# A four-layer Perceiver on one core: where the turned maxima sit in PSUM, and how the queries for the maxima are laid out

## The reference, cut to what matters

```
q = norm(x) @ Wq + bq;  k = ctx @ Wk + bk;  v = ctx @ Wv + bv        (16 heads of 16)
x = x + softmax(q k^T / 4 over 12544 keys) v @ Wo + bo
```

## Time and profile before

| | us |
|---|---|
| median of 3 runs | 1688.18 (1687.93 to 1692.31) |
| profiled execution, its own time | 1688.73 |
| its span, first to last instruction | 1686.9 |
| TensorE matmul busy | 1578.0 (94%) |
| TensorE weight loads busy | 1362.0 (81%) |
| VectorE busy | 1045.9 (62%) |
| ScalarE busy | 964.8 (57%) |
| GpSimd busy | 697.7 (41%) |

### The profile page before, as it was taken

The page is one execution under the profiler, slowest core; times in us unless marked ns, Lnnn a source line. Parts: engine busy times, 40 slices in busy tenths (PEclk is TensorE's granted clock), DMA queues, the critical chain, the costliest instruction groups (busy, mean ns, idle before and its releaser), DMA issues. The chain is left out here.

```text
span 1686.9 us, 48994 instructions
## 1 busy us (share of the span) xinstructions
PE 1578.0 (94%) x20162; PEld 1362.0 (81%) x20179; DVE 1045.9 (62%) x1445; ACT 964.8 (57%) x1848; POOL 697.7 (41%) x627
## 2 busy tenths in 40 slices
PE   6999999999887999999999987998799999999988
PEld 5888888888666889888898765986588898898863
DVE  7667777786346877777777343045676666666622
ACT  4677777777413466656656712352367777777742
POOL 5655555551004655554554000000375555555202
PEclk9999999999977999999999999999999999999998
DMA  7665555554234766555555352971475555555430
GB/s 180 166 198 131 120 140 131 132 123 106 65 116 116 183 182 170 143 145 138 137 147 126 88 207 85 362 256 51 127 175 140 138 128 120 140 133 132 100 108 4
DMA packets 149248, 235.65 MB, mean 140 GB/s; under 512 B 24200, under 2 KB 64516, under 8 KB 148100
## 3 DMA queue, kind: packets, MB, share of 16 engines
q1 hardware_dynamic: 141090, 225.29, 50.6%
q10 hardware_dynamic: 7938, 7.23, 1.7%
HBM read 107.26 MB, written 0.23 MB: 64 GB/s over the span
## 5 line engine op out<-in xcount | busy, mean ns | idle before, releaser
L1305 DVE TENSOR_REDUCE L_xattn_maxima<-L_xattn_ps 128x4 f32<-128x1024 f32 x588 | 691.6, 1219 | 327.3 <-PE L_xattn_ps L877 323.2
L1067 ACT ACTIVATE L_xattn_p_ring<-L_xattn_ps 128x512 f32<-128x512 f32 x1176 | 674.9, 599 | 340.8 <-PE L_xattn_ps L926 325.7
L926 PE MATMUL L_xattn_ps<-L_xattn_q_packed,L_xattn_k_packed 128*128 128x256 f32 x2352 | 452.1, 298 | 10.0 <-ACT L_xattn_p_ring L1067 5.0
L926 PEld LDWEIGHTS L_xattn_ps<-L_xattn_q_packed,L_xattn_k_packed 128*128 128x128 f32 x2352 | 335.3, 190 | 71.6 <-issue 35.9
L962 PE MATMUL L_xattn_ps<-L_xattn_p_ring,L_xattn_v_ring 128*17 128x128 f32 x9408 | 289.3, 273 | 1.0 <-ACT L_xattn_p_ring L1067 1.0
L962 PEld LDWEIGHTS L_xattn_ps<-L_xattn_p_ring,L_xattn_v_ring 128*17 128x17 f32 x9408 | 242.4, 97 | 23.6 <-ACT L_xattn_p_ring L1067 1.6
L845 PE MATMUL L_xattn_ps<-L_xattn_ctx_halves,L_xattn_w_halves 128*128 128x256 f32 x1764 | 260.9, 286 | 0.5 <-POOL L_xattn_ctx_halves L1224 0.4
L849 PE MATMUL L_xattn_ps<-L_xattn_w_halves,L_xattn_ctx_halves 128*128 128x256 f32 x1764 | 260.4, 286 | 0.0
L1239 POOL TENSOR_TENSOR L_xattn_k_ring<-L_xattn_k_full,consts 128x512 fp32r<-128x512 f32 x147 | 155.5, 1058 | 223.0 <-ACT L_xattn_k_full L1080 111.6
L1221 POOL TENSOR_TENSOR L_xattn_ctx_halves<-L_xattn_ctx_chunk,consts 128x512 fp32r<-128x512 f32 x129 | 134.4, 1042 | 263.1 <-DMA L_xattn_ctx_chunk<-in_ctx_chunks 178.9
L845 PEld LDWEIGHTS L_xattn_ps<-L_xattn_ctx_halves,L_xattn_w_halves 128*128 128x128 f32 x1764 | 233.3, 193 | 3.7 <-issue 1.8
(11 more groups left out here) (385 smaller groups left out, 1173.2 us busy)
## 6 DMA issues: line engine op xcount, KB each, us to landing
L_xattn_k_packed<-L_xattn_k_ring SPq DMA_DIRECT2D x588, 128.0 KB, 2.4
L_xattn_ctx_chunk<-in_ctx_chunks SPq DMA_DIRECT2D x147, 256.0 KB, 3.2
L_xattn_k_packed<-L_xattn_k_ring SPq DMA_DIRECT2D x588, 64.0 KB, 2.2
L_ffn_W<-in_experts_W SPq DMA_DIRECT2D x16, 1024.0 KB, 13.7
L_xattn_mask_chunk<-L_xattn_mask ACTq DMA_DIRECT2D x49, 128.0 KB, 3.0
weights<-in_pack_L_attn SPq DMA_DIRECT2D x10, 512.0 KB, 4.3
L_xattn_ctxT<-in_ctxT SPq DMA_DIRECT2D x5, 896.0 KB, 12.9
L_xattn_ctx<-in_ctx SPq DMA_DIRECT2D x5, 896.0 KB, 11.8
```

What stands on the lines that cost most here:

```text
L926: last = pe.matmul(L.ps[:, bank, d * 2 * S:(d + 1) * 2 * S], self.k_packed[s][:, quarter, d, half * P:(half + 1) * P], q[:, 2 * pair:2 * p ...
L1067: act.activation(self.p[t % P_RING][:, 4 * quarter:4 * quarter + 4, :], L.ps[:, E_BANK[unit], :].rearrange("p (h n) -> p h n", n=S), ACT.Exp)\
L1305: dve.tensor_reduce(out[:, 4 * v:4 * v + 4], L.ps[:, M_BANK + 2 * v:M_BANK + 2 * v + 2, :] .rearrange("p b (k n) -> p (b k) n", k=2), AX_X ...
```

## The change

1. `q_hi` and the packed source `q_pairs` hold four heads' worth (two for each block of eight) in place of 16. Within a strip's 32 rows only two heads lie, so a 0/1 column that keeps every even (or every odd) head, `pair16`, serves all four strips at once. VectorE's two products shrink from 128 x 1024 to 128 x 256, ScalarE's sixteen copies to four, its copy of 128 x 2048 to 128 x 512. The matmuls read the same numbers. The DMAs that pack the queries keep number and bytes.
2. In the turn steps from 9 to 45 of each layer (ten, `borrows(step)`) turned maxima and factor leave banks 0 and 1 and go to banks 2 and 3, where the first half of a maxima batch lies. They wait until VectorE has reduced the first half of that step's batch 0; batch 1 of the step waits until ScalarE has read the factor.
3. In those steps `pe_factor` moves from behind all six matmuls of `pe_project` part 3 to behind the first three; in all steps from 6 to 48 part 3 is issued in two calls of three. ScalarE takes the factor's exp right after unit 5 and before `act_drain_v`, not after it.

```diff
-          ("head16", 8), ("head32", 4), ("neg_half", 1), ("fill", P), ("turned", 1), ("turn_sign", 1)]
+          ("head16", 8), ("head32", 4), ("pair16", 2), ("neg_half", 1), ("fill", P), ("turned", 1), ("turn_sign", 1)]
...
+        "pair16": p[:, None] // 16 % 2 == np.arange(2)[None, :]
...
+def borrows(step):
+    return LAG <= step < NCHUNK
...
     def unit(key, step):
+        if key[0] != "scores" and borrows(step):
+            before.append(-1)
+            at[key] = len(at)
+            bank.append(M_BANK if key[0] == "turned" else M_BANK + 1)
+            return
...
-        self.q_hi = sb("q_hi", [P, H, S], F32R)
+        self.q_hi = sb("q_hi", [P, 2 * DC, S], F32R)
...
-        self.q_pairs = self.p_ring[:, 0:2, :, :]
+        self.q_pairs = self.p_ring[:, 0, :, :].rearrange("p (a h) n -> p a h n", h=2 * DC)[:, 0:2, :, :]
...
     def pe_batch(self, pe, step, d):
+        b = block_turned(step)
         pe.wait_ge(L["q_heads_ready"], d + 1)
+        if d == 1 and b and borrows(step):
+            pe.wait_ge(L["e_drained"], E_AT["factor", b] + 1)
...
-                    last = pe.matmul(bank[:, r, k * KEYS:(k + 1) * KEYS], self.q_hi[own, 8 * d + 2 * r + k, :],
+                    last = pe.matmul(bank[:, r, k * KEYS:(k + 1) * KEYS], self.q_hi[own, 2 * d + k, :],
...
     def pe_turned(self, pe, b):
-        self.pe_bank_free(pe, unit)
+        if borrows(step):
+            pe.wait_ge(L["batch_reduced"], 4 * (step - 1) + 1)
+        else:
+            self.pe_bank_free(pe, unit)
...
                 self.pe_unit(pe, m, 5)
-                self.pe_project(pe, step, 3)
+                self.pe_project(pe, step, 3, 0, 3)
                 if b:
                     self.pe_factor(pe, b)
+                self.pe_project(pe, step, 3, 3, 6)
                 self.pe_unit(pe, m, 6)
                 self.pe_batch(pe, step, 1)
...
     def act_low_queries(self, act, c):
-        for h in range(HPB):
-            last = act.activation(self.q_pairs[:, 0, c * HPB + h, :], self.qT_halves[:, 1, c, :], ACT.Copy,
-                                  scale=self.net.const("head16")[:, h:h + 1])
+        for k in range(2):
+            last = act.activation(self.q_pairs[:, 0, 2 * c + k, :], self.qT_halves[:, 1, c, :], ACT.Copy,
+                                  scale=self.net.const("pair16")[:, k:k + 1])
...
     def scalar(self, act):
-                if u == factor_before(step) and b:
+                if u == factor_before(step) and b and not borrows(step):
                     self.act_factor(act, b)
                 if u < 8:
                     self.act_unit(act, m, u)
...
+                if u == 5 and b and borrows(step):
+                    self.act_factor(act, b)
                 if u == 5:
                     self.act_drain_v(act, step)
...
     def vector(self, dve):
-            dve.tensor_tensor(self.q_hi[:, c * HPB:(c + 1) * HPB, :], times(self.qT_halves[:, 0, c, :], HPB),
-                              wide(net.const("head16"), S), ALU.mult).then_inc(L["q_heads_ready"], 1)
+            dve.tensor_tensor(self.q_hi[:, 2 * c:2 * c + 2, :], times(self.qT_halves[:, 0, c, :], 2),
+                              wide(net.const("pair16"), S), ALU.mult).then_inc(L["q_heads_ready"], 1)
```

18 lines of the change are left out of this document (10 added, 8 removed).

## The result

The changed kernel takes 1680.14 us (median of 5 runs, 1679.17 to 1682.62), the kernel before 1688.18 beside it (5 runs, 1686.62 to 1693.23). The ratio is 0.9953 with a 95% interval of 0.9934 to 0.9972: 8.0 us or 0.5% faster. The profiled execution took 1682.3 us (span 1680.5). The forecast was 1677.0, with 1669 to 1684 as the range.

A forecast was written before the change was run, and what follows sets the result against it. TensorE was taken to bound the steady steps, VectorE the layer starts. Turn steps 9.2 plus L3 1.3 plus L1 1.5 less L0 0.8 gave 11.2 us, so 1677.0 us, range 1669 to 1684.

The forecast's parts named there:

- Unit 5 and unit 7: Turn steps: idle before their weight loads goes, 0.31 for unit 5 in 30 steps, 0.26 for unit 7 in L0 and L3.
- Batch 1 waits for the factor's exp: Turn steps: a new wait of 0.15 us before batch 1, starting at T + 2.09; bounds nothing to 0.6.
- no wait at batch 1: Rival, chance 0.17: turn steps gain 14.8 - 0.3 and the starts up to 5, about 1671 us.
- The turned maxima: Turn steps: they now wait for VectorE's reduction of batch 0's first half, costing 0.3 us for all 30.
- the sign named for it: Turn steps: under 0.1 us idle before the turned maxima; above 0.3 the prediction is wrong.
- v drain: Turn steps: ends near T + 2.54, next k projection covered by 0.05; 0.6 us allowed for brushes.
- Sum of the turn steps: All 30 turn steps: 8.4 in L0 and L3 plus 1.7 in L1, less 0.3 and 0.6, gives 9.2 us.
- The stretch named as a sign: V projection to next step: 3.4 us in place of 3.84 in L0 and L3, 0.17 shorter in L1.
- L3: 1.3 forecast: L3's start: first reduction 1.9 us earlier through smaller queries, of which 1.3 survives the wait for the context chunk.
- L1: 1.5 forecast: L1's start: first reduction 0.6 earlier, more if the clock stays up; 1.5 us gained, between 0.6 and 2.2.
- L0: a loss of 0.8 forecast: L0's start: the four constants move into GpSimd's busy stretch and can wait for it, losing 0.8 us.
- Total: Whole kernel: 9.2 + 1.3 + 1.5 - 0.8 = 11.2 us gained, giving 1677.0 us.

The follow-up runs named there:

- factor ring: Changed kernel with only the turned maxima in a batch bank, the factor back in the ring of two E banks: 1672.92 us, ratio 0.9912.
- the banks alone: Changed kernel with only the borrowed banks and new factor order kept, queries for sixteen heads as before: 1686.56 us, ratio 0.9987.
- the queries alone: Changed kernel with only the smaller queries kept, turned maxima and factor placed as before: 1683.18 us, ratio 0.9964.
- the repeat: The changed kernel once more, unchanged: 1679.77 us, ratio 0.9949 to the kernel before.
- unit 7 first: Changed kernel with unit 7 issued ahead of batch 1 in the 30 turn steps: 1684.74 us, ratio 0.9966.
- context ahead: Changed kernel with SyncE's loads of context chunks 5 to 9 issued one step earlier: 1678.30 us, ratio 0.9932.
- fill the wait: Changed kernel with ten matmuls of zeros before the first turned transpose in each layer: 1680.57 us, ratio 0.9942.
- queries before keys: Ring with context, plus packing of key chunk 1 moved behind the queries and first shift in SyncE's queue: 1673.88 us, ratio 0.9893.
- v drain first: Changed kernel with ScalarE draining the values ahead of the factor's exp in the 30 turn steps: 1704.58 us, ratio 1.0094.
- ring with context: Changed kernel with the factor back in the E-bank ring and context loads one step earlier: 1668.89 us, ratio 0.9888.
- the added matmuls: Nine matmuls of zeros ahead of L1's last attention tile: on the changed kernel 1679.67 us (0.9933), on the banks alone 1684.82 us (0.9972).

## Why the prediction was right, and which terms were off

**Unit 5 and unit 7** (0.31 and 0.26 gone): right in place; the second is mis-sized. In the changed kernel batch 1 is followed by the next step's projection after 0.69 us (1265.83 to 1266.52), before after 0.79 with the wait of 0.26 in it. And in the factor ring, with no wait at all, it is 0.66. A wait of 0.26 was worth 0.13: between the end of batch 1's loads and unit 7's, 0.13 stay without a wait (1266.16 to 1266.29). Over 20 steps that is 2.6 us too much in the sum. Unit 5's loads follow T's without a gap, so there the 0.31 counted in full.

**Batch 1 waits for the factor's exp**: the chain was right within 0.1 us in each link (factor T + 0.66, forecast 0.70; exp at T + 1.36, forecast 1.40 to 1.45; batch 1 at T + 2.03, forecast 2.09). The row shows 0.27, but 0.14 of it stand there without a wait, and the factor ring gives 0.12 to 0.13 back: against the 0.15 of the forecast, right. The rival "no wait at batch 1" is the factor ring's kernel, and its steps give 11.1 us, not the 14.5 of the sum, for unit 7's reason above and because T waits there too.

**The turned maxima**: this term was mis-sized. Forecast 0.3 us for all 30; the wait is about 0.2 us in 6 of L3's ten steps, 0.1 to 0.2 in nine of L0's and 0.06 in nine of L1's (each is the distance from the v projection to T less 0.73), 3 us together. Like unit 7's, it is not worth its length: a step of L3 with a wait of 0.2 takes 3.64 and one without 3.52, one of L0 with 0.13 takes 3.58, and L1's one step without takes as long as the others. That makes some 1.4 us, 1.1 too little in the sum. I had released TensorE 0.05 behind the reduction, the figure of a release by ScalarE; by the rows it is 1.34 less a reduction of 1.22, so 0.12. And TensorE comes to T sooner, 0.73 behind the v projection and not 0.79. Both together turn the forecast's 0.05 into 0.2, and the sign named for it, under 0.1, was missed in 15 of the 20 steps of L0 and L3. Besides, the late reduction was there in three of L3's ten steps before and is in six now; why more, the runs don't say.

**v drain**: 0.6 us for brushes weren't needed; no projection waits for it (the drain ends at T + 2.45, the next projection starts at T + 2.72).

**Sum of the turn steps**: forecast 9.2; the steps give 6.7 and 7.1 in two profiles of the changed kernel, 6.3 with the banks alone. 9.2 - 2.6 - 1.1 + 0.6 is 6.1, the rest is some 0.02 to 0.03 a step that I can't place. The stretch named as a sign, 3.4 in L0 and L3, was 3.5 to 3.7, and 0.17 less in L1 was 0.19.

**Starts.** L3: 1.3 forecast, 1.5 and 1.3 measured at T9, 1.4 with the queries alone; the chunk of the context caps it as forecast. Its first reduction comes 1.8 earlier, counted from the first projection (1.9 forecast), and its two products take 0.76 (0.35 each forecast). L1: 1.5 forecast; 3.1 in the repeat, 3.0 with the queries alone, 0.3 in the first profile. Its first reduction comes 1.15 us earlier, and not 0.6. The clock stays up as the theory hoped (twelve v loads take 1.49 us from 532.99, 2.63 before). L0: a loss of 0.8 forecast, and this is wrong in sign. Three of the four constants took 0.21, 0.68 and 0.41 and only the last was held up, 1.26. I had them all meet GpSimd's instructions; they met its pause instead, 13.91 to 15.21. The constants cost no more than before, and the operations ahead of them gave some 3. By the Trainium skill (SBUF — State Buffer, "Who interferes with whom") the two engines lock each other out only while both are at work; the trace agrees: the first cast took 0.21 while GpSimd was idle, the last 1.26 beside a GpSimd instruction that runs from 15.21 for 1.29. (The third, begun at 15.19, took its usual 0.41, and the GpSimd instruction begun at 15.21 took 1.29, where the 147 of its kind have a median of 1.04.) The rule was sound; I had applied it to all four. L0 gains 2.9 with the queries alone, 1.1 and 0.1 in the changed kernel, and the queue and the clock take the rest.

**Total.** Steps 6.7 to 7.1, starts 1.9 to 5.5, less 2.4 to 5.1 between the layers, against 1686.9. The forecast of 11.2 was close to what the kernel's own parts give (8.6 to 12.6), and the measured 8.0 is that less the clock's part in a stretch that I hadn't counted at all. The clock of all executions says the same: 0.9699 against 0.9730 is some 2.3 us by the fit (an estimate), so 8.0 would be 10.3 at the clock of the kernel before. So the 3.1 us by which the forecast missed are not one error: turn steps too high by 2.3, starts too low by up to 3.5, and up to 5.1 from the clock elsewhere. These partly cancel, and that the total came so near is in part luck.

**Open.** Between the layers the changed kernel (twice), banks only, unit 7 first, context ahead, fill the wait and queries before keys take 252.2 to 255.5 us; the kernel before, queries only, v drain first, factor in ring and ring with context 249.5 to 250.2. Chance alone it is not: the kernels whose clock over all executions lies at 0.969 to 0.971 (the changed one twice, banks only, unit 7 first, context ahead) are all of the first list, and none of the second has less than 0.973. But what in a kernel's timing decides it, the runs don't show; both lists have kernels with a borrowed bank, and fill the wait and queries before keys have 253.6 and 254.8 in their profiles at 0.973. The first fall stands 22.6 to 23.6 us behind T51 in the good ones and 21.9 to 22.1 or 24.7 to 25.1 in the others; with the added matmuls it stands at 25.5 and 24.8, and less their 2.05 at 23.4 and 22.7.

## What to carry to other kernels

Idle time before a weight load is an upper bound of what its removal gives: look what stands at the same place in a step without the wait. Here half of it did. When a wait goes, ask which engine then leads, and price its release from a row of that same engine. A borrowed buffer should not be one that starts the next chain: borrowing one bank for the turned maxima gave 11 us in the turn steps (8.4 in the profile with the 2 us of VectorE in it), borrowing a second for the factor gave 7. And under about 5 us, look at a stretch with the same instructions in both profiles, and at the clock of all executions and not of the profiled one, before believing a total.

## What the runs showed of the hardware

- A reduction on VectorE releases TensorE about 0.12 us behind its end (T 1.34 behind the start of 1.22 us), an exp on ScalarE 0.05 to 0.07.
- The same instructions between L1 and L3 took 249.5 to 255.5 us at a mean granted clock of 0.96 to 0.92. Work added ahead of them (2.05 us) made them 2 to 6 us shorter, net of itself, and took the clock of the banks-only kernel over twelve executions from 0.969 to 0.973.
- A half-clock stretch of 3.4 us cost nothing in L1's T5 to T9 (34.49 against 34.43) and about 0.5 in L3's, one of 10.2 us in L1's 2.6.
- Small VectorE operations of the shift (0.17 us) took 0.96 to 1.25 beside GpSimd's back-to-back instructions, and TensorE then idled 2.1 us for the reduction behind them.
